# Cross attention over eight batches: score tiles 0 to 3 normalised on ScalarE, the fourth reciprocal ahead of the additions of the last channel tile

## The reference

```
q = einsum('bcn,dc->bnd', x, Wq) + bq          # b=8, c=512, n=1024, d=64
k = einsum('bcn,dc->bdn', ctx, Wk) + bk[:, None]
v = einsum('bcn,dc->bdn', ctx, Wv) + bv[:, None]
attn = softmax(einsum('bnd,bdm->bnm', q, k), axis=2)
out = einsum('bcm,bnm->bcn', v, attn) + x
```

## Time and profile before

| | us |
|---|---|
| median of three runs | 658.86 (658.78 to 661.23) |
| the profiled execution | 658.98 |
| its span, first to last instruction | 657.2 |
| TensorE busy | 646.6 (98%) |
| VectorE busy | 473.9 (72%) |
| ScalarE busy | 297.1 (45%) |
| GpSimd busy | 116.0 (18%) |

### The profile page before, as it was taken

One profiled execution on the slowest core, in us unless ns is written; L12 is line 12 of the kernel. 1 busy time (PEld: TensorE's weight loads), 2 busy tenths in 40 slices (PEclk: granted clock), 3 DMA queues, 4 the chain that ended last, 5 costly groups with the idle time before them and its releaser, 6 DMA issues.

```text
span 657.2 us, 8861 instructions
## 1 busy us (share of the span) xinstructions
PE 646.6 (98%) x3118; PEld 525.6 (80%) x3118; DVE 473.9 (72%) x530; ACT 297.1 (45%) x397; POOL 116.0 (18%) x50
## 2 busy tenths in 40 slices
PE   8999999999999999999999999999999999999997
PEld 5778888878787787878878788787888878888786
DVE  5897868767777677786686966869658697596641
ACT  6886533644245443374423753336623456235120
POOL 0022200431005310054000630006300053001100
PEclk9999999999999999999999999999999999999999
DMA  8903534972349632586316772177531874416352
GB/s 304 351 1 77 144 86 128 293 191 80 106 124 305 166 103 73 128 303 176 96 64 153 278 176 96 64 183 272 152 109 59 210 261 126 128 64 144 75 161 84
DMA packets 94254, 100.10 MB, mean 152 GB/s; under 512 B 7328, under 2 KB 69024, under 8 KB 94240
## 3 DMA queue, kind: packets, MB, share of 16 engines
q1 hardware_dynamic: 94240, 99.91, 51.1%
HBM read 51.64 MB, written 16.78 MB: 104 GB/s over the span
## 4 chain that ended last, share of the span: by engine, by line
PE 50%; DVE 22%; SPq 10%; issue 10%; DMA 4%; ACT 3%; ACTq 0%; DVEq 0%
PE acc_ps L944 39%; SPq L243 10%; PE s_ps L866 8%; DVE blocks L670 6%; DVE negmax L639 6%; DMA pt_raw<-blocks 3%; DVE vt_lo L573 2%; DVE pt_lo L573 2%; DVE probs L650 2%; DVE o_sb L703 1%; DVE o_sb L699 1%; ACT vt_hi L345 1%; PE s_ps L882 1%; DMA stage<-in_ctx_dram 1%; PE acc_ps L1049 1%
## 5 line engine op out<-in xcount | busy, mean ns | idle before, releaser
L944 PE MATMUL acc_ps<-pt_hi,vt_hi 128*128 128x512 f32 x442 | 173.9, 393 | 4.0 <-DVE vt_lo L573 4.0
L944 PE MATMUL acc_ps<-pt_hi,vt_lo 128*128 128x512 f32 x442 | 172.1, 389 | 0.0
L944 PE MATMUL acc_ps<-pt_lo,vt_hi 128*128 128x512 f32 x442 | 172.0, 389 | 0.0
L425 ACT ACTIVATE probs<-s_ps,negmax 128x1024 f32<-128x1024 f32 x56 | 62.5, 1117 | 133.4 <-DVE negmax L639 133.4
L308 POOL TENSOR_TENSOR pt_lo<-pt_raw,pt_hi 128x1024 fp32r<-128x1024 f32 x14 | 41.1, 2951 | 370.9 <-ACT pt_hi L345 370.9
L944 PEld LDWEIGHTS acc_ps<-pt_hi,vt_hi 128*128 128x128 f32 x442 | 82.9, 188 | 26.9 <-DVE vt_lo L573 7.0
L944 PEld LDWEIGHTS acc_ps<-pt_hi,vt_lo 128*128 128x128 f32 x442 | 83.0, 188 | 17.5
L944 PEld LDWEIGHTS acc_ps<-pt_lo,vt_hi 128*128 128x128 f32 x442 | 83.0, 188 | 16.7
L308 POOL TENSOR_TENSOR xs_lo<-stage,xs_hi 128x1024 fp32r<-128x1024 f32 x29 | 72.8, 2513 | 108.3 <-ACT xs_hi L345 107.7
L913 PE MATMUL acc_ps<-wv_hi,xs_hi 128*128 128x512 f32 x224 | 87.2, 389 | 0.0
L913 PE MATMUL acc_ps<-wv_lo,xs_hi 128*128 128x512 f32 x224 | 87.1, 389 | 0.0
(11 more groups left out here) (116 smaller groups left out, 980.5 us busy)
## 6 DMA issues: line engine op xcount, KB each, us to landing
pt_raw<-blocks SPq DMA_DIRECT2D x240, 128.0 KB, 2.4
stage<-in_x_dram SPq DMA_DIRECT2D x32, 512.0 KB, 6.3
o_sb<-in_x_dram SPq DMA_DIRECT2D x64, 256.0 KB, 3.3
out_dram<-o_sb SPq DMA_DIRECT2D x64, 256.0 KB, 2.5
stage<-in_ctx_dram SPq DMA_DIRECT2D x31, 512.0 KB, 8.8
pt_raw<-in_L_xattn_Wv_dram SPq DMA_DIRECT2D x4, 256.0 KB, 6.9
stage<-in_ctx_dram SPq DMA_DIRECT2D x2, 256.0 KB, 3.7
pt_raw<-in_L_xattn_Wk_dram SPq DMA_DIRECT2D x1, 128.0 KB, 3.6
```

The source lines that it names most:

```text
L425: nc.scalar.activation(probs[:, t % 2, :], s_ps[:, t % 2, :, :].rearrange("p a n -> p (a n)"), ACT.Exp, bias=negmax[:, t:t + 1], accum_out ...
L944: mm = nc.tensor.matmul(acc_ps[:, c % BANKS, :], v[:, m, cols], p[:, m, :], start=(m == 0 and v is vt_hi and p is pt_hi), stop=(m == MT - ...
```

## The change

ScalarE gets a new step `scale(b, t)`, called behind each of the four exponentials of tiles 0 to 3: it waits for the reciprocal and multiplies the tile in place. VectorE's `normalise` of these tiles becomes `inverse`, the reciprocal alone. `inverse(3, nb)` stands ahead of `out_rows(b, 3)`, where `normalise(nb, 3)` stood behind it. Tiles 4 to 7, batch 0, TensorE, GpSimd and SyncE keep their code.

```diff
+            def scale(b, t):
+                act.wait_ge(s_inv, b * ST + t + 1)
+                nc.scalar.activation(probs[:, t % 2, :], probs[:, t % 2, :], ACT.Copy,
+                                     scale=inv[:, t:t + 1]).then_inc(s_norm, 1)
...
                 k_high(nb)
                 for t in range(NT):
                     exp(nb, t)
+                    scale(nb, t)
...
-            def inverse(t):
-                dve.wait_ge(s_exp, t + 1)
+            def inverse(t, b=0):
+                dve.wait_ge(s_exp, b * ST + t + 1)
...
                 neg_max(nb, 0)
-                normalise(nb, 0)
+                inverse(0, nb)
                 neg_max(nb, 1)
                 turn(nb, 0)
                 out_rows(b, 2)
-                normalise(nb, 1)
+                inverse(1, nb)
                 neg_max(nb, 2)
                 turn(nb, 1)
-                normalise(nb, 2)
+                inverse(2, nb)
                 neg_max(nb, 3)
                 turn(nb, 2)
+                inverse(3, nb)
                 out_rows(b, 3)
-                normalise(nb, 3)
                 turn(nb, 3)
```

## The result

| | before | after |
|---|---|---|
| median of four runs each | 658.86 (658.78 to 661.23) | 652.18 (652.04 to 652.39) |
| the profiled execution | 658.98 | 652.31 |
| its span | 657.2 | 650.5 |
| TensorE busy | 646.6 (98%) | 645.0 (99%) |
| VectorE busy | 473.9 (72%) | 458.1 (70%) |

The ratio of after to before is 0.989, 95% interval 0.9868 to 0.9913: 1% faster. It moved the way that was forecast, by 6.7 us in place of 5.8.

The account below looks back on a forecast made before the run. TensorE, busy for 646.6 of 657.2 us, loses time only in seven vt_lo waits: 4.0 + 7 x 0.26 = 5.8 us. 658.98 - 5.8 = 653.2, taken as 653.1 us; range 652.2 to 656.5.

Parts of the forecast that it names:

- The bound and the chain: TensorE waits 4.0 us in seven batch changes for vt_lo, behind scores, transposes, sixteen transfers, then vt and pt work.
- the 1.8 us to spare: At the batch change's end, vt_lo would end near 372.2 where TensorE wants it at 374.0, instead of 0.5 late.
- The new chain, tile by tile: VectorE and ScalarE steps of tiles 0 to 3: fourth transpose ends at 347.75, transfers start 2.3 us earlier.
- The long wait: The one vt_lo wait showing 1.82 idle, 2.08 late through late-landing transfers; 2.3 us earlier covers it by a hair.
- the size of a wait: TensorE's loss per vt_lo wait: idle time shown + 0.16 + 0.10; for seven, 4.0 + 7 x 0.26 = 5.8 us.
- the 0.16 and the 0.10: Additions to a wait's idle time: 0.39 matmul length against the 0.23 pace, and the next matmul 0.33 behind, not 0.23.
- The lower end of the range: 652.2 us: no case gives back more than the waits; 0.9 below the forecast is scatter between runs.
- the first (the transfers give it back): The DMA side sets the pace, so transfers land no earlier: partly 653.8 to 656; wholly 658.9, no change or nearly 0.17.
- The second (uncovered multiplications): VectorE has nothing between reciprocal and transpose: 0.59 more per tile, 2.4 per batch change, 675.5 us; chance 0.06.
- The third (a handoff of 0.3 rather than 0.11): Slower handoff on each tile eats 0.8 of the 2.3: 653.1 to 654; with rival 1 in part, chance 0.12.
- The moved reciprocal: Fourth reciprocal ahead of channel tile 3's additions covers the multiplication; left behind them, about 1.2 us would be uncovered.

Follow-up runs that it names:

- the reordered one: Kernel before with only the reciprocal and multiplication of tile 3, both still on VectorE, moved ahead of the additions of channel tile 3: 663.7 us, ratio 1.0066.
- the uncovered one: Changed kernel with VectorE's order turned round so that nothing lies under the multiplications: 689.22 us, ratio 1.0456.
- the one with three extra instructions: Changed kernel with three useless VectorE maximum instructions (about 3.4 us) ahead of the fourth transpose in all batch changes: 664.02 us, ratio 1.0067.
- the repeated pair: Both kernels measured once more without any edit: kernel before 659.93 us (ten runs), changed kernel 652.22 us.
- The experiments with waits in one batch change: Changed kernel with useless VectorE instructions ahead of the fourth transpose in the first batch change alone: three gave 653.44 us, five gave 657.08 us.

## Why the prediction was right or wrong

**The bound and the chain: right.** TensorE's one repeated wait was the only thing to be won on this chain, and all seven went. The last vt_lo has the 1.8 us to spare that were forecast. That more isn't to be had on this chain is shown by taking nearly the whole multiplication away (652.32), and that the chain was what held TensorE, by lengthening it (652.19 with 1.1 us, 664.02 with 3.4).

**The new chain, tile by tile: right, by compensation.** The fourth transpose came 2.63 us earlier, not 2.3. Most of the difference arose on ScalarE: from the second reciprocal to the fourth I had 344.96 - 339.44 = 5.52, and it took 340.89 - 335.75 = 5.14. A multiplication starts 0.20 behind the start of its reciprocal (341.09 for 340.89), where I had 0.27, and the next exponential starts as the multiplication ends (339.66 for 338.50 + 1.15), where I had 0.12 in between. VectorE too goes on sooner behind the fourth reciprocal (340.89 to 340.97, 0.08 for my 0.19). The transfers took 0.33 more, which I had set at 0. That the sum, 2.29, is the forecast's 2.3 is luck: two errors of the same size cancelled.

**The long wait: gone, but for another reason than forecast.** The 2.3 us were said to cover it by a hair. They were never put to it, since the landing that had been late came in time. In the second batch change the last landing of the kernel before was this one (chain of waits, start, us, what), and this is the transpose of the changed kernel that waits for it:

```profile
198.36 3.99 DMA pt_raw<-blocks
```
```profile
197.90 1.25 DVE L676 STREAM_TRANSPOSE blocks<-probs 128x1024 f32<-128x1024 f32 x1 [0.74 <-DMA pt_raw<-blocks]
```

In the changed kernel that landing takes 2.45 us, as in its other batch changes. What the late ones have in common is in the view of the DMA queues. In the kernel before, between 199.7 and 202.4 us, it shows a transfer of the instruction queue, one of nine in the whole execution:

```profile
q8 instruction: 1, 0.02, 2.8%
```

Of the twelve traces, five have such a transfer between the start of the sixteen transfers and their last landing in the second batch change (the kernel before twice, the reordered one, the uncovered one, and the one with three extra instructions), and just these five have a last landing of 3.2 to 4.0 us. In the other seven it comes behind the landing, which takes 2.4 to 2.5. So the change moved the sixteen transfers out of its way, which the prediction could not know: luck. No run moves that transfer alone, so that it is the cause is likely and not shown. An estimate of what the cover was worth: the last vt_lo of that change ended at 209.95, 1.46 ahead of its matmul at 211.41; with a landing 1.5 later it would have been about 0.1 late. The hair would have been missing, and some 0.4 us lost, but not the 2.2 of before.

**The step that failed: the size of a wait, and with it the sum.** I priced a wait at its idle time + 0.26 us, which gave 5.8 for the seven. A batch took 80.07 us from wait to wait (374.56 to 454.63 in the trace of before) and takes 79.38 now, so that wait, 0.40 by the page, cost 0.69 rather than 0.66; the long one cost 81.60 - 79.38 = 2.22 rather than 2.08. Set beside one another matmul by matmul, the starts of the two traces move apart at the seven waits by 0.59, 2.22, 0.66, 0.69, 0.71, 0.69 and 0.67, together 6.23 us where the page has 4.03 idle, and nowhere else between the first wait and the last. So the 0.26 was 0.30 for an ordinary wait and 0.40 for the long one: the 0.16 and the 0.10 were there (0.16 and 0.11), but the next matmuls lost another 0.03 that I had put at nothing, and the one just ahead of the long wait was 0.09 late as well.

That is half of the miss. With 6.2 in place of 5.8 the forecast would have been 652.6, inside the range. Of the rest, 0.36 us is start-up, where the pair of traces differs (negmax 0 at 91.30 and 90.94) and which belongs to no step of the change; 0.09 came behind the last wait, at one matmul, and stays open. In the repeated pair the seven waits cost 6.37, the start-up 0.08. So that the time fell below 652.2, and not just towards it, is scatter. The lower end of the range had left 0.9 us for that, and the price of the waits had used up half of it.

**What the prediction did not see: a second level of the time before.** Of 45 runs of the kernel before made beside the experiments, 27 with a mean clock of 0.999 or more have a median of 658.73, and 18 at 0.997 of 660.43. (One of the 27, at 1.000, took 660.05; why is not known.) The changed kernel had a median of 652.22 in eight runs, never below 0.999. So the change is worth 6.5 us against the one level and 8.2 against the other. The experiments with waits in one batch change show what brings the clock down: a wait as long as the one that the prediction listed as one of seven. I had priced it as idle time only. This is shown for the made waits and, in the traces, behind the long waits of the reordered kernel, of the uncovered one and of the one with three extra instructions; in the kernel before itself it is inferred from the clock of its runs, since both of its profiled executions were at full clock.

**The rivals.** Of the first (the transfers give it back) a part was true, 0.33 of 2.63 us, too little to count. The second (uncovered multiplications) was not this kernel's case, but its mechanism is real: with the cover taken away the time was 689.2. That is well over the 675.5 that I gave it. Some 8 us of the difference are the clock's; the rest is that the fourth transpose came 3.2 us later than before (20.3 for 17.2) and not 2.4, in an order in which the next maxima come late as well. The third (a handoff of 0.3 rather than 0.11) is out: ScalarE starts 0.20 behind the start of a reciprocal that itself lasts 0.16. The Trainium skill (ScalarE: Activation LUTs, Rules for kernel authors) puts multiplications on VectorE, not ScalarE. The trace of the changed kernel agrees on the durations (817 ns for those left on VectorE, 1153 on ScalarE), but the advice would have been wrong here, where VectorE was on the chain and ScalarE was not.

**The moved reciprocal.** I wrote that it pays, and 1.2 us is what it gave VectorE. I didn't say that the time could do without it. It can: 652.29.

## What to carry to other kernels

Where one engine is busy for 98% of the span, look for the few places where it waits, and follow each back to the engine that has no gap; take work off that engine even if another does it more slowly, as long as something useful lies under it. The order decides more than the durations: the same 28 multiplications gave 652 or 689 us. Price a wait of TensorE by the distance from one matmul to the same one a batch later, not by the idle time shown, and look at the clock of every run: a long wait can be charged twice.

## What the runs showed of the hardware

- TensorE's granted clock can fall to half around a wait of about 2 us (1.8 shown idle). In the traces it fell once in the reordered kernel, five times behind the seven such waits of the uncovered one, once with three extra instructions in every batch change and once with five in one; by the mean clock it fell in seven of eight runs of the last. The fall came between 0.5 us before the end of the wait and 1.5 us after it, lasted 3.4 us each time, and cost 1.6 us by the starts of the matmuls, 1.7 by the two levels of the kernel before. Behind single waits of 0.84 us shown idle it never fell in five runs, nor in any trace behind one of up to 1.04 that no longer one followed. In the kernel before, with the same 1.8 us of idle time in both traces, it came in 18 of 45 runs; what decides between runs is open.
- The issue of the sixteen transfers of 128 KB takes 10.50 to 10.56 us when a 256 KB store and a 256 KB load were issued 2.1 us or more ahead, in all batch changes but one (11.02, in the uncovered kernel, where a transfer of the instruction queue fell among them). It takes 10.65 to 11.29 when the additions, and so the store 1.15 us ahead, stand directly before the fourth transpose (the changed kernel twice, the reordered one, and the one with nearly no multiplication).
- The last landing of the sixteen transfers of the second batch change took 3.2 to 4.0 us in the five traces in which a transfer of the instruction queue fell among them or their landing, and 2.4 to 2.5 in the other seven. That the one delays the other isn't shown by a run that changes it alone.
- A wait of TensorE costs more than the idle time that the profile shows: here 0.30 us more for a short one, 0.40 for the one of 1.8, with matmuls drawn 0.39 long at a pace of 0.23.
